# Out stage of a two-layer conditioned block: a ring of four result chunks, and stores of y issued from ScalarE

## Chip, cores and metric

One core of a Trainium2 chip runs the whole program. The metric is the device time of one execution in microseconds (us), lower is better. Before the change it is 1996.15 us, the median of 3 runs (1995.97 to 1996.78).

## What is computed

The input x has 4 batches of 1024 tokens of 512 floats, and each batch has one conditioning row. A first layer (modulated layer norm, two small two-matrix networks with gates) gives x2. A second layer normalises, attends with 16 heads, and ends like this:

```python
        out = jnp.moveaxis(out, 1, 2).reshape(B, N, D)
        out = out @ Wp.T + bp
        h1 = out + hidden
        h2 = _sln(h1, w, ln_g, ln_b, Wg, bg, Wb, bb)
        return h2 + h1
```

`_sln` takes mean and variance of each token, and scales and shifts the normalised row by two rows of its batch (gamma times the norm's own gain, and the shift). The change touches this end alone: projection, residual, layer norm, output.

## The kernel before

The program has five stages, one after the other: set-up, first layer, q/k/v, attention, and the out stage. Each stage is a block in which every engine runs a list of its own, written out by hand; the order on an engine or queue is the order of that list, and semaphores join the lists. SP (SyncE) issues nearly all DMAs. It issues them in the order of its list, so a wait in it holds back every DMA behind it.

The 4096 tokens are cut into 8 chunks (NCH) of 512 tokens, each of 4 tiles (TT) of 128 tokens. In the out stage (`out_stage`, L1490 to L1640), for chunk s and tile t:

- **TensorE** (`project_chunk`) writes the projected tile to a PSUM bank: a bias matmul (L61) and 12 matmuls (L67), since the float32 product is split into three. Chunk 0 is projected at the end of the attention stage. A bank comes free when VectorE has read it two chunks before.
- **VectorE** runs, in its loop over tiles, `add_residual` (L1568: PSUM plus the residual tile gives h1), the statistics (L1570), `centre` of the same tile number in the chunk before (L1579: (h1 - mean) * scale row into z), the aggregation of statistics (L1574), and `finish` of that same earlier tile (L1585: z * rstd + h1t, the result, in place in z). So VectorE adds chunk s and finishes chunk s-1, and after the last add it centres and finishes the four tiles of chunk 7.
- **GpSimd** makes rstd from the variances (L1621, L1623) and h1t = h1 + shift row (L1630).
- **SP** loads, for each chunk, the attended values (`load_attended`, L101, four DMAs into o_a) and the residual (`load_residual`, L107, o_x), both in rings of 4 chunks (A_RING). Chunks 0 and 1 and the style rows of batches 0 and 1 (`load_style`, L113) are loaded already in the attention stage. Chunks 2 to 5 are loaded at the start of the out stage, chunk s+4 once chunk s was projected and its h1 made. SP also stores the results (L1540, one 1 MB DMA for a chunk; L1555, four of 256 KB for chunk 7) and loads the style rows of batches 2 and 3, each behind a store.
- **ScalarE** has no list in this stage.

z has 2 chunk buffers. `output_ready` (L1588) makes VectorE wait, ahead of the first `centre` of chunk s, for the store of chunk s-2 (`z_free`), for the style rows and for rstd. The SP list reads: loads of chunk 4; loads of 5, store 0; loads of 6, store 1, style rows of batch 2; loads of 7, store 2; store 3, style rows of batch 3; stores 4 to 6; the four tiles of chunk 7.

Of the kernel before, what the change touches and what calls it, by code (L numbers as in the profile page):

```python
# [6 lines left out]
P = 128  # L7
B, N, D = 4, 1024, 512
# [6 lines left out]
NCH = T // CH  # L15
TT = CH // P
# [6 lines left out]
A_RING = 4  # L23
# [55 lines left out]
def early(nc, *specs):  # L79

    with ExitStack() as ctx:
        return [ctx.enter_context(nc.sbuf_tensor(*spec)) for spec in specs]
# [13 lines left out]
def load_attended(eng, sh, s):  # L98

    for k in range(KT):  # L100
        eng.dma_start(sh.projection_a[s % A_RING][:, k].bitcast(F32),  # L101
                      sh.at_d[KT * (s // QH) + k, s % QH]).then_inc(sh.a_loaded[s % A_RING], 16)
# [7 lines left out]
def load_style(eng, sh, b):  # L110

    for i in range(2):
        eng.dma_start(sh.style[:, b % 2, i], sh.rows_d[2 + i, b].partition_broadcast(P)).then_inc(sh.st_loaded[b % 2], 16)  # L113
# [887 lines left out]
def attention_stage(nc, sh, wp_t):  # L1001
# [11 lines left out]
    with ExitStack() as ctx:  # L1013
# [17 lines left out]

        x01, a23, a01, x23, sh.style = early(nc, *PROJECTION_TILES)
        sh.projection_a = [a01[:, 0], a01[:, 1], a23[:, 0], a23[:, 1]]
# [397 lines left out]
        def _(pool):  # L1431
# [14 lines left out]
            def group(g, slot, nth=None, first=False, load=True, with_next=True):  # L1446

                for pair in range(PAIRS if with_next else PAIRS - 1):
# [33 lines left out]

PROJECTION_TILES = (("o_x01", [P, 2, TT, D], F32), ("o_a23", [P, 2, KT, 2, CH], F32R), ("o_a01", [P, 2, KT, 2, CH], F32R),
                    ("o_x23", [P, 2, TT, D], F32), ("o_style", [P, 2, 2, D], F32))
PROJECTION_WORDS = 2 * 2 * TT * D + 2 * 2 * KT * 2 * CH + 2 * 2 * D
# [2 lines left out]
def out_stage(nc, sh, y_out):  # L1490

    with ExitStack() as ctx:  # L1494
        def sb(name, shape, dt=F32):
            return ctx.enter_context(nc.sbuf_tensor(name, shape, dt))

        def sem(name):
            return ctx.enter_context(nc.semaphore(name))

        sb("o_tiles_place", [P, PROJECTION_WORDS])
        h1 = sb("o_h1", [P, 2, TT, D])
        h1t = sb("o_h1t", [P, TT, D])
        z = sb("o_z", [P, 2, TT, D])
        stats = sb("o_stats", [P, TT, 6])
        mv = sb("o_mv", [P, 2, TT, 2])
        ve = sb("o_ve", [P, TT])
        rstd = sb("o_rstd", [P, 2, TT])

        x_loaded, st_loaded = sh.x_loaded, sh.st_loaded  # L1510
        p_done, h1_ready = sh.p_done, sh.h1_ready
        stats_ready, mv_ready = sem("o_stats_ready"), sem("o_mv_ready")
        ve_ready, rstd_ready = sem("o_ve_ready"), sem("o_rstd_ready")
        centred, h1t_ready, y_ready = sem("o_centred"), sem("o_h1t_ready"), sem("o_y_ready")
        z_free = [sem("o_z_free0"), sem("o_z_free1")]

        y_v = y_out.rearrange("(s t p) d -> s p t d", s=NCH, p=P)
        LAST = NCH - 1

        block = ctx.enter_context(nc.Block())  # L1520

        @block.sync
        def _(sp):
            def load_chunk(s):
                if s >= A_RING:

                    sp.wait_ge(p_done, TT * (s - A_RING + 1))
                if s == LAST - 1:

                    for half in range(QH):  # L1530
                        sp.wait_ge(sh.out_free[half], 16 * (G + 1))
                load_attended(sp, sh, s)
                if s >= A_RING:
                    sp.wait_ge(h1_ready, TT * (s - A_RING + 1))
                load_residual(sp, sh, s)

            def store(s):

                sp.wait_ge(y_ready, TT * (s + 1))
                sp.dma_start(y_v[s], z[:, s % 2]).then_inc(z_free[s % 2], 16)  # L1540

            for s in range(2, A_RING):
                load_chunk(s)
            for s in range(LAST):
                if s + A_RING < NCH:
                    load_chunk(s + A_RING)
                if s >= 1:
                    store(s - 1)
                if s % 2 == 0 and 2 <= s < NCH - 2:
                    load_style(sp, sh, s // 2 + 1)  # L1550
            store(LAST - 1)

            for t in range(TT):
                sp.wait_ge(y_ready, TT * LAST + t + 1)
                sp.dma_start(y_v[LAST][:, t], z[:, LAST % 2, t]).then_inc(z_free[LAST % 2], 16)  # L1555
            sp.wait_ge(z_free[0], 16 * NCH // 2)
            sp.wait_ge(z_free[1], 16 * (NCH // 2 - 1 + TT))

        @block.tensor
        def _(pe):  # L1560
            for s in range(1, NCH):
                project_chunk(pe, sh, s)

        @block.vector
        def _(dve):
            def add_residual(s, t):
                dve.wait_ge(p_done, TT * s + t + 1)
                nc.vector.tensor_tensor(h1[:, s % 2, t, :], sh.ps[4 * (s % 2) + t][:], sh.projection_x[s % A_RING][:, t, :], ALU.add).then_inc(h1_ready, 1)  # L1568
                dve.wait_ge(h1_ready, TT * s + t + 1)
                nc.vector.bn_stats(stats[:, t, :], h1[:, s % 2, t, :]).then_inc(stats_ready, 1)  # L1570

            def aggregate(s, t):
                dve.wait_ge(stats_ready, TT * s + t + 1)
                nc.vector.bn_aggr(mv[:, s % 2, t, :], stats[:, t, :]).then_inc(mv_ready, 1)  # L1574

            def centre(s, t):

                dve.wait_ge(mv_ready, TT * s + t + 1)
                nc.vector.scalar_tensor_tensor(z[:, s % 2, t, :], h1[:, s % 2, t, :], mv[:, s % 2, t, 0:1],  # L1579
                                               sh.style[:, s // 2 % 2, 0], ALU.subtract, ALU.mult).then_inc(centred, 1)  # L1580

            def finish(s, t):
                dve.wait_ge(centred, TT * s + t + 1)
                dve.wait_ge(h1t_ready, TT * s + t + 1)
                nc.vector.scalar_tensor_tensor(z[:, s % 2, t, :], z[:, s % 2, t, :], rstd[:, s % 2, t:t + 1], h1t[:, t, :],  # L1585
                                               ALU.mult, ALU.add).then_inc(y_ready, 1)

            def output_ready(s):  # L1588

                dve.wait_ge(st_loaded[s // 2 % 2], 32 * (s // 4 + 1))  # L1590
                if s >= 2:
                    dve.wait_ge(z_free[s % 2], 16 * (s // 2))
                dve.wait_ge(rstd_ready, s + 1)

            for s in range(NCH):
                dve.wait_ge(x_loaded[s % A_RING], 16 * (s // A_RING + 1))
                for t in range(TT):
                    add_residual(s, t)
                    if s == LAST and t == TT - 1:
                        aggregate(s, t)  # L1600
                    if s >= 1:
                        if t == 0:
                            output_ready(s - 1)
                        centre(s - 1, t)
                    if s < LAST or t < TT - 1:
                        aggregate(s, t)
                    if s >= 1:
                        finish(s - 1, t)
            for t in range(TT):
                if t == 0:  # L1610
                    dve.wait_ge(z_free[LAST % 2], 16 * (LAST // 2))
                centre(LAST, t)
            dve.wait_ge(rstd_ready, NCH)
            for t in range(TT):
                finish(LAST, t)

        @block.gpsimd
        def _(pool):
            def inv_std(s):
                pool.wait_ge(mv_ready, TT * (s + 1))  # L1620
                nc.gpsimd.tensor_tensor(ve[:], mv[:, s % 2, :, 1], sh.eps[:, 1], ALU.add).then_inc(ve_ready, 1)  # L1621
                pool.wait_ge(ve_ready, s + 1)
                nc.gpsimd.tensor_tensor(rstd[:, s % 2], ve[:], sh.minus_half[:], ALU.pow).then_inc(rstd_ready, 1)  # L1623

            def add_shift(s, t, after):
                pool.wait_ge(h1_ready, TT * s + t + 1)
                if after > 0:

                    pool.wait_ge(y_ready, after)
                nc.gpsimd.tensor_tensor(h1t[:, t, :], h1[:, s % 2, t, :], sh.style[:, s // 2 % 2, 1], ALU.add).then_inc(h1t_ready, 1)  # L1630

            for s in range(LAST):
                inv_std(s)
                pool.wait_ge(st_loaded[s // 2 % 2], 32 * (s // 4 + 1))
                for t in range(TT):
                    add_shift(s, t, TT * s + t if s < LAST - 1 else TT * (s - 1) + t + 1)
            for t in range(TT):
                if t == TT - 1:
                    inv_std(LAST)
                add_shift(LAST, t, TT * (LAST - 1) + t + 1)  # L1640
# [109 lines left out]
```

## Time and profile before

| | us |
|---|---|
| median of 3 runs | 1996.15 |
| the profiled execution's own time | 1994.75 |
| its span in the trace | 1992.6 |
| out stage on VectorE, first instruction to the end of the last | 1884.50 to 1989.99 |
| TensorE clock granted, mean of the execution | 0.972 |

Times in the trace count from the start of the span. The last 108 us are the out stage; the 1884 us ahead of it run the same instructions in both kernels. "Idle before" in a row of the timeline is the time in which the engine stood still before that instruction, with what ended it in brackets. A landing time is that from a DMA's issue until its semaphore says that it is done.

### The profile page before, as it was taken

The numbers are of one execution on the slowest core, as the hardware profiler recorded it, in microseconds if no ns is written. First come the engines' busy times: TensorE is split into PE (matmuls) and PEld (weight loads), VectorE is DVE, ScalarE is ACT, GpSimd is POOL, SyncE is SP. The second block draws the span as 40 slices with busy tenths as digits, with TensorE's granted clock in tenths as the row PEclk, the third lists the DMA queues.
The fourth block names the chain that finished last, engine by engine and source line by source line (L and its number), as shares of the span: only waits on it lengthen the run. The fifth ranks groups of instructions, "written<-read, shape, count | busy, mean of one in ns | idle before, by whom it ended". The sixth has DMA issues, their size and how long they took to land. (4 is left out here: it accounts for less than half of the span.)

```text
span 1992.6 us, 31072 instructions
## 1 busy us (share of the span) xinstructions
PE 1902.4 (95%) x10520; PEld 1243.4 (62%) x10520; DVE 1209.5 (61%) x1510; ACT 809.2 (41%) x1373; POOL 1147.9 (58%) x589
## 2 busy tenths in 40 slices
PE   6599999999998999998999999999999999999995
PEld 1478888888886888885445544554554545554584
DVE  3556555655646554446666666666666666664289
ACT  1322123112312222221566656666666666666300
POOL 0574465466445121212477777777777777877545
PEclk9799999999999999997899999999999999999997
DMA  6301110101123555566344422344443334405293
GB/s 240 123 1 53 45 41 21 53 32 39 35 74 101 190 188 181 189 198 175 73 97 108 103 67 77 96 102 98 107 103 78 78 83 102 107 24 181 92 392 123
DMA packets 117704, 212.67 MB, mean 107 GB/s; under 512 B 18599, under 2 KB 36135, under 8 KB 117577
## 3 DMA queue, kind: packets, MB, share of 16 engines
q1 hardware_dynamic: 98828, 200.04, 33.7%
q10 hardware_dynamic: 18560, 10.94, 1.9%
q8 instruction: 78, 1.28, 0.3%
q14 instruction: 46, 0.37, 0.1%
q0 software_dynamic: 192, 0.05, 0.0%
HBM read 134.40 MB, written 75.80 MB: 105 GB/s over the span
## 5 line engine op out<-in xcount | busy, mean ns | idle before, releaser
L1371 DVE TENSOR_REDUCE at_mrow<-banks 128x1 f32<-128x1024 f32 x512 | 604.4, 1217 | 281.2 <-PE banks L1204 281.2
L1349 ACT ACTIVATE at_probs<-banks 128x512 f32<-128x512 f32 x1024 | 557.6, 597 | 333.7 <-PE banks L1220 314.4
L1468 POOL TENSOR_TENSOR at_pair<-at_probs 128x2048 f32<-128x2048 f32 x127 | 582.0, 4583 | 176.8 <-ACT at_probs L1349 176.7
L1220 PE MATMUL banks<-early_qs,early_ks 98*128 98x512 f32 x1024 | 443.8, 436 | 5.5 <-ACT at_probs L1349 5.5
L1204 PE MATMUL banks<-early_ks,early_qs 96*128 96x512 f32 x1024 | 377.5, 413 | 13.3 <-DVE at_mrow L1371 9.7
L1220 PEld LDWEIGHTS banks<-early_qs,early_ks 98*128 98x128 f32 x1024 | 192.4, 189 | 211.6 <-ACT at_probs L1349 106.8
L1232 PE MATMUL banks<-at_probs,at_v 128*32 128x512 f32 x2048 | 274.9, 609 | 0.9 <-ACT at_probs L1349 0.9
L1204 PEld LDWEIGHTS banks<-early_ks,early_qs 96*128 96x128 f32 x1024 | 199.1, 197 | 53.4 <-DVE at_mrow L1371 26.7
L67 PE MATMUL banks<-l_ht,l_weights 128*128 128x512 f32 x768 | 178.8, 392 | 5.5 <-ACT l_gt L574 5.5
L67 PE MATMUL banks<-qk_nt,l_weights 128*128 128x512 f32 x768 | 177.1, 392 | 3.0 <-ACT qk_gt L889 3.0
L67 PE MATMUL banks<-l_weights,l_hf 128*128 128x512 f32 x768 | 177.3, 390 | 0.0
L574 ACT ACTIVATE l_gt<-banks,mod 128x512 f32<-128x512 f32 x64 | 48.1, 778 | 314.3 <-PE banks L468 278.7
L67 PEld LDWEIGHTS banks<-l_ht,l_weights 128*128 128x128 f32 x768 | 144.6, 189 | 35.6 <-issue 5.8
L67 PEld LDWEIGHTS banks<-qk_nt,l_weights 128*128 128x128 f32 x768 | 145.3, 189 | 33.5 <-ACT qk_gt L889 3.2
L67 PEld LDWEIGHTS banks<-l_weights,l_hf 128*128 128x128 f32 x768 | 143.7, 188 | 29.5
L1248 PEld LDWEIGHTS banks<-at_pair,at_ones_col 128*32 128x32 f32 x2032 | 66.3, 110 | 138.9 <-issue 133.0
L1248 PE MATMUL banks<-at_pair,at_ones_col 128*32 128x256 f32 x2032 | 151.1, 381 | 0.0
L988 POOL TENSOR_TENSOR qk_nt<-qk_gt,qk_nt 128x512 fp32r<-128x512 f32 x32 | 43.0, 1363 | 156.2 <-DVE qk_nt L940 156.2
L898 ACT ACTIVATE qk_out<-banks,cols 128x512 fp32r<-128x512 f32 x64 | 44.1, 690 | 192.5 <-PE banks L67 186.4
L700 POOL TENSOR_TENSOR l_ht<-l_gt,l_ht 128x512 fp32r<-128x512 f32 x64 | 84.3, 1318 | 62.7 <-DVE l_ht L616 62.7
L583 ACT ACTIVATE l_gt<-banks,cols 128x512 f32<-128x512 f32 x96 | 64.7, 689 | 105.0 <-POOL l_hf L700 51.0
L700 POOL TENSOR_TENSOR l_hf<-l_gt,l_hf 128x512 fp32r<-128x512 f32 x64 | 82.7, 1293 | 40.6 <-DVE l_hf L616 40.6
(120 smaller groups left out, 1955.3 us busy)
## 6 DMA issues: line engine op xcount, KB each, us to landing
qk_scratch<-qk_out SPq DMA_DIRECT2D x64, 512.0 KB, 2.8
early_ks<-qk_scratch SPq DMA_DIRECT2D x48, 512.0 KB, 6.7
early_qs<-qk_scratch SPq DMA_DIRECT2D x96, 256.0 KB, 11.6
attn_scratch<-at_out SPq DMA_DIRECT2D x32, 512.0 KB, 2.7
o_a<-attn_scratch SPq DMA_DIRECT2D x32, 512.0 KB, 11.0
v_scratch<-qk_v ACTq DMA_DIRECT2D x32, 256.0 KB, 2.4
at_v<-v_scratch SPq DMA_DIRECT2D x16, 512.0 KB, 14.6
o_x<-x_scratch SPq DMA_DIRECT2D x8, 1024.0 KB, 14.3
```

The source lines that it names most:

```text
L67: last = pe.matmul(out, stationary(a), moving(b), start=start and n == 0, stop=stop and n == len(TERMS) - 1)
L574: nc.scalar.activation(gt[:, k % 2, :], half[k][:], ACT.Identity, bias=sh.mod[:, 2 * which + 1, k, bass.ds(b, 1)], scale=sh.mod[:, 2 * whi ...
L583: nc.scalar.activation(gt[:, n % 2, :], halves[n][:], func, bias=sh.cols[:, col + m:col + m + 1]).then_inc(gt_full, 1)
L700: nc.gpsimd.tensor_tensor(dst[:, LO, i, :], gt[:, i % 2, :], dst[:, HI, i, :].bitcast(F32), ALU.subtract).then_inc(gt_lo, 1)
L898: nc.scalar.activation(qk[:, m, HI, :], ps[m][:], ACT.Identity, bias=sh.cols[:, C_BQ + m:C_BQ + m + 1]).then_inc(qk_hi, 1)
L1204: pe.matmul(e_ps[u % 2][:, keys, :], qs[0:96, slot, half, j, c * P:(c + 1) * P], ks[0:96, slot, j, keys * CH:(keys + 1) * CH], start=True, ...
L1220: pe.matmul(et[j % 2][:], ks[0:98, slot, j, (i % KC) * P:(i % KC + 1) * P], qs[0:98, slot, i // KC, j, :], start=True, stop=True).then_inc ...
L1232: last = pe.matmul(av_ps[rows, :], v[:, slot, kc, rows], probs[:, kc % 4, j, :], start=kc == 0, stop=kc == KC - 1)
L1248: last = pe.matmul(den_ps[HD * j:HD * (j + 1), cols], ones_col[:], psum2[:, pair % 2, j, cols], start=n == 0 and part == 0, stop=n == KC / ...
L1349: nc.scalar.activation(probs[:, i % 4, j, :], et[j % 2][:], ACT.Exp).then_inc(exp_done, 1)
L1371: nc.vector.tensor_reduce(mrow[:, half, u:u + 1], e_ps[u % 2], AX.XY, ALU.max).then_inc(max_done, 1)
L1468: nc.gpsimd.tensor_tensor(psum2[:, pair % 2], probs[:, a], probs[:, a + 1], ALU.add).then_inc(pair_ready, 1)
```

## The change

z gets four chunk buffers (Z_RING = 4) instead of two, each with a semaphore of its own, so that `centre` of chunk s waits for the store of chunk s-4. All stores of y, and the style rows of batches 2 and 3, are issued from ScalarE's queue; SP keeps the loads of chunks 2 to 7. The four waits for the last stores are ScalarE's too. z grows from 16 to 32 KB in each partition.

```diff
+Z_RING = 4
...
-        z = sb("o_z", [P, 2, TT, D])
+        z = sb("o_z", [P, Z_RING, TT, D])
...
-        z_free = [sem("o_z_free0"), sem("o_z_free1")]
+        z_free = [sem(f"o_z_free{i}") for i in range(Z_RING)]
...
-            def store(s):
-
-                sp.wait_ge(y_ready, TT * (s + 1))
-                sp.dma_start(y_v[s], z[:, s % 2]).then_inc(z_free[s % 2], 16)
-
             for s in range(2, A_RING):
                 load_chunk(s)
+            for s in range(NCH - A_RING):
+                load_chunk(s + A_RING)
+
+        @block.scalar
+        def _(act):
             for s in range(LAST):
-                if s + A_RING < NCH:
-                    load_chunk(s + A_RING)
-                if s >= 1:
-                    store(s - 1)
-                if s % 2 == 0 and 2 <= s < NCH - 2:
-                    load_style(sp, sh, s // 2 + 1)
-            store(LAST - 1)
-
+                act.wait_ge(y_ready, TT * (s + 1))
+                act.dma_start(y_v[s], z[:, s % Z_RING]).then_inc(z_free[s % Z_RING], 16)
+                if s in (1, 3):
+                    load_style(act, sh, s // 2 + 2)
             for t in range(TT):
-                sp.wait_ge(y_ready, TT * LAST + t + 1)
-                sp.dma_start(y_v[LAST][:, t], z[:, LAST % 2, t]).then_inc(z_free[LAST % 2], 16)
-            sp.wait_ge(z_free[0], 16 * NCH // 2)
-            sp.wait_ge(z_free[1], 16 * (NCH // 2 - 1 + TT))
+                act.wait_ge(y_ready, TT * LAST + t + 1)
+                act.dma_start(y_v[LAST][:, t], z[:, LAST % Z_RING, t]).then_inc(z_free[LAST % Z_RING], 16)
+            for i in range(Z_RING):
+                act.wait_ge(z_free[i], 16 * (NCH // Z_RING + (TT - 1 if i == LAST % Z_RING else 0)))
...
             def output_ready(s):
 
                 dve.wait_ge(st_loaded[s // 2 % 2], 32 * (s // 4 + 1))
-                if s >= 2:
-                    dve.wait_ge(z_free[s % 2], 16 * (s // 2))
+                if s >= Z_RING:
+                    dve.wait_ge(z_free[s % Z_RING], 16 * (s // Z_RING))
                 dve.wait_ge(rstd_ready, s + 1)
```

In `centre`, `finish` and the last wait of VectorE, `s % 2` and `LAST // 2` become `s % Z_RING` and `LAST // Z_RING` for z; nothing else changes on VectorE, TensorE or GpSimd.

## Rows read from the trace of the kernel before

**Rows 1.** The page's first part: busy time, share of the span, instructions.

```profile
PE 1902.4 (95%) x10520; PEld 1243.4 (62%) x10520; DVE 1209.5 (61%) x1510; ACT 809.2 (41%) x1373; POOL 1147.9 (58%) x589
```

**Rows 2.** Busy time by stretch: length, busy time by engine, granted clock, DMA share, GB/s.

```profile
1908.60:1916.00 7.40, 7.40 (x34) 6.03 (x33) 7.30 (x15) 0.00 (x0) 4.03 (x4) 1.00 1.03 402
1922.30:1940.00 17.70, 17.70 (x79) 14.42 (x77) 17.44 (x31) 0.00 (x0) 9.28 (x8) 1.00 1.02 378
```

**Rows 3.** The waits from 1820 on: us in total, times, longest.

```profile
DVE o_z L1579 <- DMA y<-o_z: 7.1, 2, 5.9
```

**Rows 4.** Timeline of VectorE in the out stage: start, length, instruction, idle before.

```profile
1890.62 0.67 DVE L1568 TENSOR_TENSOR o_h<-banks,o_x 128x512 f32<-128x512 f32 x1
...
1902.93 0.68 DVE L1568 TENSOR_TENSOR o_h<-banks,o_x 128x512 f32<-128x512 f32 x1
1904.26 1.73 DVE L1579 SCALAR_TENSOR_TENSOR o_z<-o_h,o_mv,o_style 128x512 f32<-128x512 f32 x1
...
1915.02 0.68 DVE L1568 TENSOR_TENSOR o_h<-banks,o_x 128x512 f32<-128x512 f32 x1
1922.32 0.75 DVE L1579 SCALAR_TENSOR_TENSOR o_z<-o_h,o_mv,o_style 128x512 f32<-128x512 f32 x1 [5.89 <-DMA y<-o_z]
...
1932.12 0.68 DVE L1568 TENSOR_TENSOR o_h<-banks,o_x 128x512 f32<-128x512 f32 x1
...
1944.20 0.68 DVE L1568 TENSOR_TENSOR o_h<-banks,o_x 128x512 f32<-128x512 f32 x1
1946.81 0.75 DVE L1579 SCALAR_TENSOR_TENSOR o_z<-o_h,o_mv,o_style 128x512 f32<-128x512 f32 x1 [1.20 <-DMA y<-o_z]
...
1956.60 0.68 DVE L1568 TENSOR_TENSOR o_h<-banks,o_x 128x512 f32<-128x512 f32 x1
...
1968.70 0.68 DVE L1568 TENSOR_TENSOR o_h<-banks,o_x 128x512 f32<-128x512 f32 x1
...
1987.26 2.73 DVE L1585 SCALAR_TENSOR_TENSOR o_z<-o_z,o_rstd,o_h1t 128x512 f32<-128x512 f32 x4
```

**Rows 5.** Timeline of GpSimd beside the first slow centre.

```profile
1904.14 1.30 POOL L1630 TENSOR_TENSOR o_h1t<-o_h,o_style 128x512 f32<-128x512 f32 x1
```

**Rows 6.** Timeline of TensorE: tile 0 of chunk 1, first of chunk 4, last.

```profile
1884.73 2.92 PE L67 MATMUL banks<-wp,o_a 128*128 128x512 f32 x12
...
1920.42 0.39 PE L61 MATMUL banks<-bias_rows,ones 128*128 128x512 f32 x1
...
1965.55 2.93 PE L67 MATMUL banks<-wp,o_a 128*128 128x512 f32 x12
```

**Rows 7.** The loads of o_a for chunk 4: issue ns, issue times, landing us.

```profile
L101 SPq DMA_DIRECT2D o_a<-attn_scratch x4: 636/1624/2787, 1889.7 to 1893.7; - x4
DMA to landing us min/median/max: 14.2/14.6/15.5
```

**Rows 8.** The store of chunk 0.

```profile
L1540 SPq DMA_DIRECT2D y<-o_z x1: 922/922/922, 1905.7 to 1905.7; - x1
DMA to landing us min/median/max: 16.6/16.6/16.6
```

**Rows 9.** The store of chunk 2.

```profile
L1540 SPq DMA_DIRECT2D y<-o_z x1: 394/394/394, 1932.2 to 1932.2; - x1
DMA to landing us min/median/max: 14.5/14.5/14.5
```

**Rows 10.** The style rows of batch 2, second of the two loads.

```profile
L113 SPq DMA_DIRECT2D o_style<-rows_scratch x1: 434/434/434, 1923.6 to 1923.6; - x1
DMA to landing us min/median/max: 12.6/12.6/12.6
```

**Rows 11.** The page's DMA issues: KB each, median us from issue to landing.

```profile
v_scratch<-qk_v ACTq DMA_DIRECT2D x32, 256.0 KB, 2.4
y<-o_z SPq DMA_DIRECT2D x4, 256.0 KB, 2.1
```

More of the change, by code:

```diff
@@ L1578, in centre @@
                 dve.wait_ge(mv_ready, TT * s + t + 1)
-                nc.vector.scalar_tensor_tensor(z[:, s % 2, t, :], h1[:, s % 2, t, :], mv[:, s % 2, t, 0:1],
+                nc.vector.scalar_tensor_tensor(z[:, s % Z_RING, t, :], h1[:, s % 2, t, :], mv[:, s % 2, t, 0:1],
                                                sh.style[:, s // 2 % 2, 0], ALU.subtract, ALU.mult).then_inc(centred, 1)
@@ L1584, in finish @@
                 dve.wait_ge(h1t_ready, TT * s + t + 1)
-                nc.vector.scalar_tensor_tensor(z[:, s % 2, t, :], z[:, s % 2, t, :], rstd[:, s % 2, t:t + 1], h1t[:, t, :],
+                nc.vector.scalar_tensor_tensor(z[:, s % Z_RING, t, :], z[:, s % Z_RING, t, :], rstd[:, s % 2, t:t + 1], h1t[:, t, :],
                                                ALU.mult, ALU.add).then_inc(y_ready, 1)
@@ L1610, in _ @@
                 if t == 0:
-                    dve.wait_ge(z_free[LAST % 2], 16 * (LAST // 2))
+                    dve.wait_ge(z_free[LAST % Z_RING], 16 * (LAST // Z_RING))
                 centre(LAST, t)
```

## The prediction, made before the changed kernel ran

> **What bounds the kernel now.** I began with the busy times. TensorE is busy for 95% of the span and VectorE for 61% [rows 1]; that average is no guide here, since it is made by 1884 us of other stages that the change does not touch. So I went to the stretches of the out stage. There TensorE and VectorE are both busy nearly all the time at a granted clock of 1.00, and the 16 DMA engines are full too, at 402 GB/s and 378 GB/s [rows 2]. Three resources look like the limit at once, and only the order of events tells which one sets the end.
>
> The timelines give it. TensorE ends tile 0 of chunk 1 at 1884.73 + 2.92 = 1887.65 [rows 6], and VectorE adds it only at 1890.62 [rows 4], 3.0 us late. TensorE's last matmuls end at 1965.55 + 2.93 = 1968.48 [rows 6], while VectorE at 1968.70 is only adding tile 0 of chunk 7 and ends its last finish at 1987.26 + 2.73 = 1989.99 [rows 4]. TensorE never has to wait for VectorE; VectorE is behind it from the first tile to the last. The end of the kernel is VectorE's end plus one store. The last store takes 2.1 us to land [rows 11], which from 1989.99 gives 1992.1 of the span of 1992.6. **VectorE's list, from its start at 1884.50, sets the time.** What shortens the out stage is what takes time out of that list.
>
> The waits say what is in it that is no work: 7.1 us in two waits, both for a store of y, both ahead of the scale-and-centre step [rows 3]. The timeline places them: 5.89 us ahead of the centre at 1922.32, and 1.20 us ahead of that at 1946.81 [rows 4]. In the code the first is the first centre of chunk 2, which reuses the buffer of chunk 0. Store 0 was issued at 1905.7 and took 16.6 us, so it landed at 1922.3 [rows 8], when VectorE went on. The second is chunk 4 behind store 2: 1932.2 + 14.5 = 1946.7 [rows 9].
>
> **What one stall is worth.** Not its own length. I took the step from the first add of a chunk to the first add of the next [rows 4]. Chunk 2 to 3: 1915.02 - 1902.93 = 12.09. Chunk 3 to 4, which holds the first stall: 1932.12 - 1915.02 = 17.10. Chunk 4 to 5: 12.08. Chunk 5 to 6, with the second stall: 1956.60 - 1944.20 = 12.40. Chunk 6 to 7: 12.10. So the stall of 5.89 costs 17.10 - 12.09 = 5.01 us and the stall of 1.20 costs 12.40 - 12.09 = 0.31 us. The rest of each is given back, and the rows show where. In a step without a stall the first centre of the chunk is slow, 1.73 us at 1904.26 against 0.75 us [rows 4], while GpSimd makes the first shift add of the same chunk (1904.14 for 1.30 us) [rows 5]. After a stall that add is long over and the centre takes 0.75 us. Without the stall the collision is back: 1.73 - 0.75 = 0.98 us. Hence I don't subtract 7.1 us but 5.01 + 0.31 = **5.3 us**.
>
> **The change, part by part.**
> 1. Four z buffers. Centre of chunk 2 and of chunk 3 wait for no store. Centre of chunk 4 waits for store 0 instead of store 2. It comes after the first add of chunk 5, at about 1944.2 - 5.0 = 1939.2, and store 0, even at the 16.6 us that it takes now, is in by 1922.3 [rows 8]: some 17 us to spare. Each later one has its store two chunks, about 24 us, further back than now. Both waits go: -5.3 us. Two more semaphores and 16 KB more in each partition cost no instruction.
> 2. Stores on ScalarE's queue. ScalarE has no work in the stage (0.00 us in both stretches) [rows 2], so its waits hold up nobody's arithmetic. Seven stores of 1 MB, four of 256 KB and four style loads leave SP, 15 issues in all, and none is issued for more. Store 0 can go at about 1903.0, when its last tile is finished right before the add at 1902.93 [rows 4], instead of 1905.7 behind the loads of chunk 5. Nothing waits for it any more: 0.
> 3. Loads on SP alone. Loads of chunks 6 and 7 no longer queue behind stores 0 and 1 and the style rows, and go by the projection of chunks 2 and 3 and their adds. TensorE waits for none of them today, so going earlier gains 0. Could they land later, as stores now flow beside them? The tightest I bound is o_a of chunk 4: last issue 1893.7, at most 15.5 us, so in at 1909.2, and TensorE begins the chunk at 1920.42 [rows 6, 7]. That is 11.2 us to spare. Stores 0 and 1 together are 2 MB, at 402 GB/s [rows 2] 5.2 us. Even if all of that came ahead of a load, 6 us are left: 0. The cover is TensorE's ring of four chunks; if it were gone, a late load would reach the end only after eating VectorE's lag of 3.0 us as well.
> 4. Style rows of batch 2 behind store 1 on ScalarE's queue. They were issued last at 1923.6 and in at 1936.2 [rows 10]; they are wanted by GpSimd and VectorE for chunk 4, about 1939 after the change. Store 1 goes when chunk 1 is finished, right before the add at 1915.02, so these go some 1916 to 1919, and with 12.6 us (to 16.6 us, the longest landing in my rows) they are in by 1932 to 1936. 3 us or more to spare: 0.
> 5. The last store. Issued by ScalarE instead of SP. This trace shows no store of y from ScalarE; the nearest rows are stores of 256 KB, median landing 2.4 us from ScalarE's queue against 2.1 us from SP's [rows 11]. The destinations differ, so I read it as a bound: 0 to +0.3 us, or as much the other way. I take 0, since size and shape of these four stores stay those of the 2.1 us row.
>
> On part 3, the stretches show the 16 engines full while one queue feeds them, so a second queue adds no bytes per second [rows 2]. The Trainium skill, "DMA: Bandwidth & Descriptors", section "Queues, rings and completion order", says that each DMA engine goes round robin between the queues that have work, a packet at a time. By it a store beside loads would take half the rate, so the stores land sooner than now and the loads later, which speaks against this part; here it moves loads by the bytes of two stores at the most, inside the spare time above. The trace of before, with one busy queue, can't show it.
>
> **Sum.** Against the profiled execution: span 1992.6 - 5.3 = 1987.3, time 1994.75 - 5.3 = 1989.4. That execution lies 1.4 us under the median of the three runs; I take the same difference from the median: 1996.15 - 5.3 = **1990.8 us**. About 0.2%, here 4.0 us, is what a measurement can tell from no change, so the forecast (0.27%) is only just past that.
>
> **Rivals.**
> - **Part of the gain is taken back by VectorE itself.** With the stall gone VectorE and GpSimd keep step throughout, and more instructions of the one may fall on the other. Each such collision costs 0.98 us as above. For it: the collision already ate 1.8 us of the 7.1. Against: the three later steps without a stall (12.09, 12.08, 12.10) differ by 0.02 us, so the pattern is settled. Two further collisions give 5.3 - 2.0 = 3.3 us and 1992.8 us. Chance 0.13.
> - **The style rows come late (slower).** Their place is ScalarE's queue behind store 1, with SP's loads beside them. VectorE's centre of chunk 4 started at 1946.81 before; only if they land after that is the kernel slower, 31 us after their issue at about 1916, against 12.6 us now. At 1950 it would be 3.2 us slower than before, about 1999.3 us. The same form holds for a load starved past its spare time. Against: 3 us to spare at least, and the order of bytes hardly changes. Chance 0.04.
> - **No effect.** Another wait ends at the same moment as the removed one: the residual of the chunk, or rstd. Then 1996 us. Against: VectorE resumed within 0.1 us of store 0's and store 2's landing, and no other wait of the centre appears in the steps without stalls. Chance 0.03.
>
> **How the numbers follow.** The forecast has 0.80. It is faster by over 0.2% whenever the gain is above 4.0 us, which the full gain is with 1.3 us in hand; of its 0.80 I give 0.02 to a measurement that falls inside the bound. Faster 0.79 (0.78 and 0.01 of the first rival), within 0.2% 0.17 (0.12, 0.03 and 0.02), slower 0.04. Low end: the whole 7.1 us is gained, no collision comes back, 1989.05, so 1989.0. High end: the first rival's 1992.8 with 0.2 us for the last store, 1993.0. The other two rivals, 0.07, stay outside, with the spread of three runs as the rest.
>
> **What would show it.** In the changed trace no wait of the centre for a store of y; six steps between first adds, each 12.1 us (the first 12.3); a slow first centre, 1.6 to 1.7 us, in chunk 2 and chunk 4; VectorE's last finish at 1984.7 and the span's end near 1987.3; TensorE without idle time, still ending at 1968.5; o_a of chunk 4 in before 1920. Wrong if VectorE waits for style rows or a residual, if TensorE stands still at the start of a chunk, or if a step takes 13 us with no wait in it, which is the collision.

## The result, and the profile after

| | before | after |
|---|---|---|
| median, 10 runs each | 1996.06 us | 1990.78 us |
| the profiled execution's own time | 1994.75 us | 1991.3 us |
| its span | 1992.6 us | 1989.2 us |

The ratio is 0.9975, with a 95% interval of 0.9965 to 0.9984: faster by 5.3 us, which is 0.26%.

The profiled execution of the kernel after lies 0.5 us above its median, that of before 1.3 us below its own. So the two spans (3.4 us apart) must not be compared as they are. The out stage begins with VectorE's first add, at 1884.50 before and at 1886.24 after; these 1.74 us lie in stages whose instructions are the same in both kernels. In the traces of the experiments below the first add lies between 1885.74 and 1886.65, also where the kernel keeps two buffers and SP's queue, so the difference isn't the change's. I count from the first add on.

The waits on VectorE from 1820 on, kernel after. The two waits for a store [rows 3] have no row any more. What is left is the entry of the stage (6.5 us until TensorE has ended chunk 0, as before) and 0.2 us for the first rstd:

```profile
DVE o_h L1565 <- PEq L1013: 6.5, 1, 6.5
DVE o_z L1576 <- POOL o_rstd L1620: 0.2, 1, 0.2
```

The timeline of VectorE after, with the rows that answer to [rows 4]: first add of chunks 1 to 7, the first centres of chunks 1, 2 and 4, the last finish.

```profile
1892.36 0.67 DVE L1565 TENSOR_TENSOR o_h<-banks,o_x 128x512 f32<-128x512 f32 x1
...
1904.69 0.68 DVE L1565 TENSOR_TENSOR o_h<-banks,o_x 128x512 f32<-128x512 f32 x1
...
1906.02 1.73 DVE L1576 SCALAR_TENSOR_TENSOR o_z<-o_h,o_mv,o_style 128x512 f32<-128x512 f32 x1
...
1916.78 0.68 DVE L1565 TENSOR_TENSOR o_h<-banks,o_x 128x512 f32<-128x512 f32 x1
...
1918.11 1.73 DVE L1576 SCALAR_TENSOR_TENSOR o_z<-o_h,o_mv,o_style 128x512 f32<-128x512 f32 x1
...
1928.88 0.69 DVE L1565 TENSOR_TENSOR o_h<-banks,o_x 128x512 f32<-128x512 f32 x1
...
1940.98 0.68 DVE L1565 TENSOR_TENSOR o_h<-banks,o_x 128x512 f32<-128x512 f32 x1
...
1942.42 1.62 DVE L1576 SCALAR_TENSOR_TENSOR o_z<-o_h,o_mv,o_style 128x512 f32<-128x512 f32 x1
...
1953.05 0.68 DVE L1565 TENSOR_TENSOR o_h<-banks,o_x 128x512 f32<-128x512 f32 x1
...
1965.14 0.69 DVE L1565 TENSOR_TENSOR o_h<-banks,o_x 128x512 f32<-128x512 f32 x1
...
1983.80 2.73 DVE L1582 SCALAR_TENSOR_TENSOR o_z<-o_z,o_rstd,o_h1t 128x512 f32<-128x512 f32 x4
```

The differences of neighbouring starts give the table:

| from first add of chunk ... to ... | before | after |
|---|---|---|
| 1 to 2 | 12.31 | 12.33 |
| 2 to 3 | 12.09 | 12.09 |
| 3 to 4 (wait of 5.89 before) | 17.10 | 12.10 |
| 4 to 5 | 12.08 | 12.10 |
| 5 to 6 (wait of 1.20 before) | 12.40 | 12.07 |
| 6 to 7 | 12.10 | 12.09 |
| 7 to the end of the last finish | 21.29 | 21.39 |
| whole, from the first add of chunk 0 | 105.49 | 100.29 |

The two steps with waits are shorter by 5.00 and 0.33 us, the tail is longer by 0.10 and the other steps by 0.03, and the sum is 5.20 us. The centres at 1918.11 and 1942.42 are those that waited before and then took 0.75 us; now they take 1.73 and 1.62 us. So about 1.9 us of the 7.1 came back as slow centres, much as the steps of the kernel before had said.

TensorE's last matmuls, kernel after: they end at 1967.29 + 2.93 = 1970.22, 1.74 us later than before [rows 6], as its start is. TensorE waited for nothing in the stage but its entry.

```profile
1967.29 2.93 PE L67 MATMUL banks<-wp,o_a 128*128 128x512 f32 x12
```

The stores of chunks 0, 1 and 2 and the loads of chunk 6 and of the residual of chunk 5, kernel after (issue ns, issue times; landing in us in the line below each):

```profile
L1547 ACTq DMA_DIRECT2D y<-o_z x1: 385/385/385, 1904.8 to 1904.8; - x1
DMA to landing us min/median/max: 10.0/10.0/10.0
...
L1547 ACTq DMA_DIRECT2D y<-o_z x1: 401/401/401, 1916.9 to 1916.9; - x1
DMA to landing us min/median/max: 10.5/10.5/10.5
...
L1547 ACTq DMA_DIRECT2D y<-o_z x1: 401/401/401, 1929.0 to 1929.0; - x1
DMA to landing us min/median/max: 12.2/12.2/12.2
...
L101 SPq DMA_DIRECT2D o_a<-attn_scratch x4: 809/1082/3262, 1910.4 to 1915.7; - x4
DMA to landing us min/median/max: 16.1/16.7/17.4
...
L107 SPq DMA_DIRECT2D o_x<-x_scratch x1: 1719/1719/1719, 1906.5 to 1906.5; - x1
DMA to landing us min/median/max: 19.7/19.7/19.7
```

This is what I had not looked at closely enough. Store 0 takes 10.0 us where it took 16.6 [rows 8], and store 2 takes 12.2 where it took 14.5 [rows 9]. The ring needs the landing of a store only within the time from the last finish of a chunk to the first centre two chunks later. Before, that was from 1903.0 to 1916.35, 13.3 us. Stores that land in 10 to 12.2 us fit into it **with two z chunks**. So the change holds two remedies for one wait, and its result can't say which of them works. The experiments take them apart.

### The profile page after: what moved, and what is told of

Read it like the earlier page. It is cut to its first block and busy times, and to the rows that moved or that the text cites. A ratio compares the mean times of both kernels' runs of the same rounds, so it can differ in the third digit from the quotient of the medians.

```text
span 1989.2 us, 31071 instructions
## 1 busy us (share of the span) xinstructions
PE 1904.1 (96%) x10520; PEld 1244.2 (63%) x10520; DVE 1213.0 (61%) x1510; ACT 809.3 (41%) x1373; POOL 1147.7 (58%) x589
## 5 line engine op out<-in xcount | busy, mean ns | idle before, releaser
L1204 PE MATMUL banks<-early_ks,early_qs 96*128 96x512 f32 x1024 | 377.6, 413 | 13.3 <-DVE at_mrow L1371 7.4
L616 DVE CAST l_ht<-l_gt 128x512 fp32r<-128x512 f32 x64 | 52.0, 812 | 90.1 <-ACT l_gt L583 49.1
```

Of the source, the lines that this page charges most:

```text
L616: nc.vector.tensor_copy(dst[:, HI, i, :], gt[:, i % 2, :]).then_inc(gt_hi, 1)
L1204: pe.matmul(e_ps[u % 2][:, keys, :], qs[0:96, slot, half, j, c * P:(c + 1) * P], ks[0:96, slot, j, keys * CH:(keys + 1) * CH], start=True, ...
```

## The experiments

All were timed beside the kernel before: 1996.22 us (24 runs) for the first four, 1995.5 us (15 runs) for the last two.

### Only the ring

```diff
 the kernel before, with
-        z = sb("o_z", [P, 2, TT, D])
+        z = sb("o_z", [P, Z_RING, TT, D])
```

Z_RING is 4, z_free has four semaphores, and the waits and buffer numbers go by Z_RING as in the changed kernel.

> Only the ring: four result chunks, stores and style rows stay in SyncE's list as before. Theory A (the ring takes the two waits away, the queue is worth nothing): no wait of the centre for a store, VectorE's out stage 5.2 to 5.3 us shorter (first add to last finish 105.5 -> 100.3 us), 1990.8 us, although store 0 still takes about 16.6 us to land. Theory B (it is the second queue, on which stores landed in 10.0 to 12.2 us instead of 14.5 to 16.6, that matters, and the ring is not needed): would still allow the gain here, but says that the next kernel has it too. Against both: if SyncE's list itself held something back (loads of chunks 6 and 7 behind stores), the gain is below 4 us.

Measured: 1990.89 us, ratio 0.9972 (0.9962 to 0.9983). No wait of the centre for a store; from the first add (1886.11) to the end of the last finish (1986.40) 100.29 us, the same as with the whole change. The stores land as late as ever, in 16.7 us, 16.4 us and, for store 2, 17.8 us:

```profile
L1541 SPq DMA_DIRECT2D y<-o_z x1: 1307/1307/1307, 1931.1 to 1931.1; - x1
DMA to landing us min/median/max: 17.8/17.8/17.8
```

The ring alone is enough. With it, that SP's list mixes loads and stores costs nothing that these times show.

### Only the queue

```diff
 the changed kernel, with
-Z_RING = 4
+Z_RING = 2
```

> Only the queue: two result chunks as before, stores and style rows from ScalarE. Between the end of the last finish of a chunk and the first centre that needs its buffer lie 13.3 us (1903.0 to 1916.35 before). Theory A of the prediction (the queue is worth nothing beyond the earlier issue of store 0, 1903 instead of 1905.7; landing time stays 14.5 to 16.6 us): store 0 lands near 1919 on the clock of before, so a wait of 3 us stays in chunk 2, and waits of 1 to 3 us come to the others: 1993 to 1995 us. Theory B (a second queue gets its turn with the loads, stores land in 10 to 12.2 us as in the changed kernel): all land inside 13.3 us, no wait of the centre, the whole gain without the ring, 1990.8 us.

Measured: 1990.8 us, ratio 0.9975 (0.9966 to 0.9984), 100.28 us from first add to last finish. The timeline shows the first centre of chunk 2 with no wait, though its buffer is the one that chunk 0 left. Store 0 was in at 1904.7 + 10.0 = 1914.7, 3.4 us before that centre:

```profile
L1547 ACTq DMA_DIRECT2D y<-o_z x1: 385/385/385, 1904.7 to 1904.7; - x1
DMA to landing us min/median/max: 10.0/10.0/10.0
...
1918.08 1.61 DVE L1576 SCALAR_TENSOR_TENSOR o_z<-o_h,o_mv,o_style 128x512 f32<-128x512 f32 x1
```

The queue alone is enough too. My prediction put the queue at 0. That is right behind the ring, which had already taken all that there was; it is wrong as a statement about the queue by itself. The tightest store is that of chunk 2, with 12.3 us against the 13.3 us that the ring of two allows.

### Neither: another order on SP

```diff
 the kernel before, with
             for s in range(LAST):
-                if s + A_RING < NCH:
-                    load_chunk(s + A_RING)
                 if s >= 1:
                     store(s - 1)
                 if s % 2 == 0 and 2 <= s < NCH - 2:
                     load_style(sp, sh, s // 2 + 1)
+                if s + A_RING < NCH:
+                    load_chunk(s + A_RING)
```

> Neither part: two result chunks, all on SyncE, but each store (and the style rows behind it) stands ahead of the loads of the next chunk in the list, so store 0 is issued at about 1903 before the loads of chunk 5 and store 1 before those of chunk 6. If a store's landing time is the bytes in front of it in its own queue: store 0 has some 7.5 us less in front of it and lands in about 9 to 12 us, store 1 likewise; store 2 (issued about 1927) has the loads of chunk 6 in front, 8 to 12 us; no wait over 1 us, 1990.8 to 1991.5 us. If stores to HBM take 14 to 16 us whatever stands in front while the engines are full: waits of 1 to 3 us at chunks 2, 3 and 4, 1994 to 1997 us. Loads of chunk 5, now issued from 1903.5, are wanted at 1932: no wait of TensorE in either case.

Measured: 1990.8 us, ratio 0.9973 (0.9964 to 0.9982), 100.26 us from first add (1885.76) to last finish (1986.02). The stores of chunks 0, 1 and 2 land in 11.7, 9.9 and 11.4 us, on the same queue of SP on which they had taken 16.6, 16.4 and 14.5 us; the first and the third of them:

```profile
L1540 SPq DMA_DIRECT2D y<-o_z x1: 395/395/395, 1904.3 to 1904.3; - x1
DMA to landing us min/median/max: 11.7/11.7/11.7
...
L1540 SPq DMA_DIRECT2D y<-o_z x1: 394/394/394, 1928.5 to 1928.5; - x1
DMA to landing us min/median/max: 11.4/11.4/11.4
```

On SP's queue, what moved the landing is the bytes in front of the store. The loads of a chunk are 3 MB (four times 512 KB and 1 MB), by my estimate 7.8 us at 402 GB/s [rows 2]. With one chunk's loads behind the store instead of in front, stores 0 and 1 land 30.2 and 40.5 us after the first add, where it was 37.8 and 48.3: 7.6 and 7.8 us earlier. For store 0, 2.6 us of that are an earlier issue and 4.9 us a shorter landing time; for store 1 the landing time is shorter by 6.5 us. The change's whole gain is there without a byte of memory and without a second queue. The loads of chunks 5, 6 and 7 now start 6.0, 8.7 and 3.6 us later, counted from the first add, and still kept TensorE supplied: it shows no wait but that of its entry.

The bytes in front on its own queue aren't all there is: on ScalarE's queue nothing stood in front of store 0, and it took 10.0 us beside SP's loads against 4.3 us for the stores of chunks 5 and 6, when no loads were left.

### What the wait hid: the slow centre

```diff
 the changed kernel, with (the same in the kernel before for the second of the two)
-                nc.gpsimd.tensor_tensor(h1t[:, t, :], h1[:, s % 2, t, :], sh.style[:, s // 2 % 2, 1], ALU.add).then_inc(h1t_ready, 1)
+                w = 1 if t == 0 and 1 <= s < LAST else D
+                nc.gpsimd.tensor_tensor(h1t[:, t, :w], h1[:, s % 2, t, :w], sh.style[:, s // 2 % 2, 1, :w], ALU.add).then_inc(h1t_ready, 1)
```

> The changed kernel, but GpSimd's first shift add of chunks 1 to 6 (tile 0) makes one column instead of 512: that part of h1t is left out, with all semaphores kept. Theory (the slow first centre, 1.73 against 0.75 us, is GpSimd's add beside it): the first centres of chunks 1 to 6 take 0.75 us, steps between first adds fall from 12.1 to 11.1 us until VectorE has used up its lag of 3.4 us behind TensorE, then 11.97 us, VectorE's last finish some 3 to 4 us earlier, 1986.5 to 1988 us. Rival (the slow centre comes from rstd or from the start of a chunk on VectorE): the first centres stay at 1.7 us, steps 12.1 us, 1990.8 us.

The cut leaves out 511 of the 512 columns of these tiles of h1t; this kernel serves only to price the collision.

Measured: 1986.6 us, ratio 0.9953 (0.994 to 0.9967); 4.2 us below the changed kernel's 1990.78, a comparison across two sets of runs. The timeline of VectorE, with GpSimd's narrow add ahead of it:

```profile
1905.39 0.19 POOL L1628 TENSOR_TENSOR o_h1t<-o_h,o_style 128x1 f32<-128x1 f32 x1
1905.51 0.75 DVE L1576 SCALAR_TENSOR_TENSOR o_z<-o_h,o_mv,o_style 128x512 f32<-128x512 f32 x1
...
1915.30 0.68 DVE L1565 TENSOR_TENSOR o_h<-banks,o_x 128x512 f32<-128x512 f32 x1
...
1926.43 0.68 DVE L1565 TENSOR_TENSOR o_h<-banks,o_x 128x512 f32<-128x512 f32 x1
...
1960.84 0.69 DVE L1565 TENSOR_TENSOR o_h<-banks,o_x 128x512 f32<-128x512 f32 x1 [0.21 <-PE banks L67]
```

The centre takes 0.75 us, the step is 1926.43 - 1915.30 = 11.13 us, and by chunk 7 VectorE waits 0.21 us for TensorE. Rstd is made as before, so the slow centre is GpSimd's add and not rstd. In the changed kernel the add of 1905.90 ends at 1907.20 and the centre of 1906.02 ends 0.55 us after it, at 1907.75. The adds and statistics of VectorE, which have one tile in SBUF as input, keep their 0.68 and 0.69 us beside the same GpSimd work (chunk 2's second tile). The rows are the changed kernel's, from its two timelines:

```profile
1905.90 1.30 POOL L1627 TENSOR_TENSOR o_h1t<-o_h,o_style 128x512 f32<-128x512 f32 x1
...
1908.45 0.68 DVE L1565 TENSOR_TENSOR o_h<-banks,o_x 128x512 f32<-128x512 f32 x1
1909.17 0.69 DVE L1567 BATCH_NORM_STATS2 o_stats<-o_h 128x6 f32<-128x512 f32 x1
...
1908.68 1.30 POOL L1627 TENSOR_TENSOR o_h1t<-o_h,o_style 128x512 f32<-128x512 f32 x1 [1.48 <-DVE o_z L1582]
```

The same cut in the kernel before:

> The kernel before, with the same cut as in the narrow-add kernel (GpSimd's first shift add of chunks 1 to 6 makes one column; that part of h1t is left out). Theory (the wait for store 0 ends when the store has landed, whatever VectorE did before, so time saved ahead of it is swallowed): the first add of chunk 4 stays 47.6 us behind that of chunk 0, the wait at chunk 2 grows from 5.9 to about 7.0 us, the wait at chunk 4 from 1.2 to about 2 us; only the 0.98 us of chunk 6's step or so reaches the end: 1994.5 to 1995.5 us, where the same cut is worth 4.2 us in the changed kernel. Rival (each of six collisions costs its 0.98 us here too, since TensorE is 8 us ahead): 1990 to 1991.5 us.

Measured: 1994.04 us, ratio 0.9993 (0.9984 to 1.0002). The waits on VectorE, and the row of the first:

```profile
DVE o_z L1579 <- DMA y<-o_z: 9.1, 2, 7.2
...
1924.77 0.75 DVE L1579 SCALAR_TENSOR_TENSOR o_z<-o_h,o_mv,o_style 128x512 f32<-128x512 f32 x1 [7.16 <-DMA y<-o_z]
```

The waits grew from 7.1 to 9.1 us, and the first add of chunk 4 (1934.55) lies 47.90 us behind that of chunk 0 (1886.65), where it lay 47.62 before. What VectorE saved ahead of a landing, it waited. In the profiled executions the stage is 1.5 us shorter than before (104.02 us, to the last finish at 1990.67), against 4.8 us for the same cut in the changed kernel (1885.74 to 1981.23, against 100.29). Both ranges were stated for a kernel before at 1996, so I read them as gains: 0.5 to 1.5 us by the theory, 4.5 to 6 by the rival. Beside its own 1995.5 the gain is 1.5 us, with an interval from 3.2 us faster to 0.4 us slower. The rival is outside it and falls; how much of the 1.5 us is real stays open.

### A version that uses it

Two z chunks, stores from ScalarE; VectorE centres and finishes five tiles behind its add instead of four; GpSimd makes h1t one tile behind the add, next to VectorE's add and statistics, and rstd after the last of the chunk. h1t has two chunks, and the style rows of batches 2 and 3 have a tile of their own, loaded at the start of the stage. The first part of the diff is VectorE's loop, the second GpSimd's; put_out centres a tile, end_with finishes it:

```diff
+LAG = 5
...
+            for n in range(TT * NCH):
+                s, t = n // TT, n % TT
...
+                add_residual(s, t)
...
+                if n >= LAG:
+                    put_out(n - LAG)
...
+                if n >= LAG:
+                    end_with(n - LAG)
...
+                add_shift(s, t, min(n + 1 - LAG, TT * NCH - 1 - LAG))
                 if t == TT - 1:
...
+                    inv_std(s)
```

> A whole kernel that tries to use what the narrow-add run showed. Two z chunks, stores from ScalarE, VectorE centres and finishes a tile five tiles (not four) behind its add, GpSimd's shift adds run one tile behind the add, each beside VectorE's add and statistics, rstd one tile later, h1t in 8 tiles, the style rows of batches 2 and 3 in a tile of their own loaded at the start of the stage. Theory (the collision is the shift add beside a step with two operands in SBUF; without it VectorE runs at 11.1 us a chunk, catches TensorE and then goes at its 11.97 us): VectorE's last add ends within 1.5 us of TensorE's last tile instead of 7, and with 1.4 us more work behind it the last finish comes 4.5 to 5.5 us before that of the changed kernel: 1985.5 to 1986.5 us. Rival (the collisions only move to other steps, since GpSimd has the same work to do): steps of 12 to 12.1 us with slow centres or finishes elsewhere, and the longer tail makes it 1991 to 1993 us.

Measured: 1984.64 us, ratio 0.9948 (0.9935 to 0.9962) to the kernel before; 6.1 us below the changed kernel's median of 1990.78, a comparison across two sets of runs. Its profiled execution was the slowest of its five (1986.4 us); there the stage takes 95.34 us (1886.64 to 1981.98) against 100.29, which is 4.95 us less. Two neighbouring first adds, and the one centre in each chunk that is still slow, with GpSimd's add beside it:

```profile
1926.41 0.68 DVE L1571 TENSOR_TENSOR o_h<-banks,o_x 128x512 f32<-128x512 f32 x1
...
1930.52 1.46 DVE L1582 SCALAR_TENSOR_TENSOR o_z<-o_h,o_mv,o_style 128x512 f32<-128x512 f32 x1
...
1938.30 0.68 DVE L1571 TENSOR_TENSOR o_h<-banks,o_x 128x512 f32<-128x512 f32 x1
```

```profile
1928.52 0.75 DVE L1588 SCALAR_TENSOR_TENSOR o_z<-o_z,o_rstd,o_h1t 128x512 f32<-128x512 f32 x1
...
1928.63 1.52 POOL L1636 TENSOR_TENSOR o_rstd<-o_ve,minus_half 128x4 f32<-128x4 f32 x1
1930.13 1.30 POOL L1643 TENSOR_TENSOR o_h1t<-o_h,o_style 128x512 f32<-128x512 f32 x1
```

The stage's 4.95 us lie inside the 4.5 to 5.5 that I had expected, the median came out a little better, and the way to both is other than I wrote. The step is 11.89 us, not 11.1: rstd, which I had counted at 1.0 us, takes 1.52 us where it starts 0.1 us after a finish, and the next add then runs beside a centre (1.46 us instead of 0.75). VectorE never waited for TensorE; it came within 0.6 us of it at the last tile (add at 1971.18, TensorE done at 1970.62). What I had not counted in the expectation is the tail. There the changed kernel has, besides the slow first centre, three more slow steps from GpSimd's five adds in a row, and its last four centres take 3.74 us; this one has one more slow centre (1.72 us at 1972.73), and its last four take 2.73 us. The rival was right about one thing: in each chunk a collision remains, at another place.

## Why the prediction was right, step by step

- **The bound.** VectorE's list sets the end: held. TensorE's end stayed where it was relative to the start of the stage, and all of the gain is in two steps of VectorE.
- **The worth of the stalls.** Predicted 5.01 + 0.31 = 5.32 us; measured 5.00 + 0.33, less 0.10 in the tail and 0.03 in the other steps, 5.20 us in the profiled stage and 5.3 us in the medians. Taking the step's excess and not the wait's 7.1 us was the choice that made the number. The narrow add shows the reason directly. The Trainium skill, "SBUF — State Buffer", section "SBUF: two separate sides", has VectorE and GpSimd share one pair of ports as an exclusive lock, which a VectorE operation with two SBUF inputs takes against a GpSimd operation that reads SBUF. The trace agrees: the centres that start inside a whole add end 0.55 us after it, and the operations with one SBUF input aren't slowed. The 0.55 us are less than the 0.75 us of a centre alone, so a small part of the centre did run beside the add.
- **Part 1, the ring.** Both waits go: held, and shown alone.
- **Part 2, the queue.** This is where the prediction fell short, without harm to the sum. I took from it 2.7 us of earlier issue and nothing else, and counted with the landing of 16.6 us. It came to 10.0 us, and the part alone brings the whole gain. The sum doesn't depend on which of the two parts does the work, so that it came out right says nothing for this reading. The sentences behind part 5 named the mechanism (stores sooner, loads later) and I did not carry it back to part 2: 16.6 us less the 7.8 us of one chunk's loads is, as an estimate, 8.8 us, under the 13.3 us that two buffers allow.
- **Part 3, the loads.** They did land later, o_a of chunk 6 in 16.1 to 17.4 us against 10.2 to 14.1 before, and the cover held: no wait of TensorE. The Trainium skill's round robin between queues ("DMA: Bandwidth & Descriptors", "Queues, rings and completion order") agrees in direction with both halves of that, 10.0 against 16.6 us for the store and longer loads beside it. In size it doesn't come to the half of the rate that the prediction drew from it: 1 MB in 10.0 us from issue to landing is 105 GB/s, of some 400.
- **Part 4, the style rows.** Issued last at 1917.9 and in after at most 14.9 us, 1932.8, wanted by GpSimd at 1942.19: 9 us to spare where I had 3 at least.
- **Part 5, the last store.** 2.1 us from ScalarE as from SP: 0, held.
- **What it should look like.** No waits, steps of 12.1 us and slow first centres of 1.6 to 1.7 us are all there. VectorE's last finish (1984.7) and the span's end (1987.3) were put in the clock of the profiled execution of before and came out 1.8 and 1.9 us later, nearly all of it ahead of the stage.
- **The rivals.** No further collision came: the same four slow steps of the tail took 0.10 us more in all, against the rival's 2.0. The late style rows and a wait in place of the removed one didn't come.

## What to carry to other kernels

When a buffer's reuse waits for a store, set three times beside each other: when the bytes were ready, what stood in front of them on their queue, and when the buffer is wanted. If they fit once the loads are moved behind, reorder the list before paying for a larger ring or another queue. Cost a removed stall by the excess of the step that holds it over one that doesn't, since the stall may cover a collision, and expect an edit upstream of a stall to be worth nothing until the stall is gone: the same cut was worth 4.2 us after the change, and before it 1.5 us, which isn't clear of zero.

## What the runs showed of the hardware that I had not expected

With the 16 DMA engines full, a store of 1 MB took 16.4 to 17.8 us behind the loads of its own queue (kernel before and the ring alone, stores 0 and 1; with the ring alone, also store 2), 10.0 to 12.3 us on a second queue beside the same loads, and 9.9 to 11.7 us on the first queue ahead of them. What the engines moved hardly changed: from 1890 to 1935 it was 391 GB/s before, 395 after, and 388 with the other order. GpSimd's operation on 4 elements in each partition (rstd) is not of fixed length: 1.02 us in most chunks, and 1.52 us in the last chunk and in the five-tile kernel from chunk 1 on, each time started 0.1 us after a finish of VectorE.
